# A 16-batch layer of two attentions and a routed feed-forward on one core: SyncE's, GpSimd's and the side jobs' order laid out anew, root-mean-square scaling moved to ScalarE and GpSimd

## The reference

```python
xn = layernorm(x)
# plain attention: 16 heads of 8, no rotation
q, k, v = split(xn @ Wqkv.T)
out_a = softmax_clipped(q @ k.T / sqrt(8)) @ v @ Wout.T   # exp(clip(s - max, -50, 50))
# rope attention and feed-forward
q, k, v = rope(xn @ Wq), rope(xn @ Wk_c @ Wk), xn @ Wv_c @ Wv
x1 = rmsnorm(xn + softmax(q @ k.T / sqrt(8)) @ v @ Wo, norm1_w)
shared = swiglu(x1 @ W_shared_in) @ W_shared_out
# group of experts by softmax, top 2 of 4 in the group, weights w
routed = sum(swiglu(x1 @ W1_shared) @ W2[e] * w[:, e] for e in range(8))
out_f = rmsnorm(x1 + shared + routed, norm2_w)
return x + out_a + out_f
```

## Time and profile before

| | |
|---|---|
| median of three runs | 2199.28 us (2190.82 to 2200.78) |
| the profiled execution | 2193.28 us, of which 2191.5 us lie between first and last instruction |
| PE busy | 1929.2 us (88%), 10244 instructions |
| DVE busy | 1688.0 us (77%), 2933 |
| ACT busy | 1439.5 us (66%), 2967 |
| POOL busy | 1082.4 us (49%), 1663 |

### The profile page before, as it was taken

The page is one execution under the profiler, slowest core; times in us unless marked ns, Lnnn a source line. Parts: engine busy times, 40 slices in busy tenths (PEclk is TensorE's granted clock), DMA queues, the critical chain, the costliest instruction groups (busy, mean ns, idle before and its releaser), DMA issues.

```text
span 2191.5 us, 43869 instructions
## 1 busy us (share of the span) xinstructions
PE 1929.2 (88%) x10244; PEld 580.1 (26%) x10244; DVE 1688.0 (77%) x2933; ACT 1439.5 (66%) x2967; POOL 1082.4 (49%) x1663
## 2 busy tenths in 40 slices
PE   5888889898898989989898998989899898998985
PEld 1122222222222222222222222222222222222222
DVE  4888978878788887978878787777878888787612
ACT  1376766676666767666676766667666676766752
POOL 2343537264563726446373653726455372644635
PEclk7599999999999999999998999999999999999998
DMA  3122221212112121212212112121211212121010
GB/s 101 37 60 65 59 69 53 71 46 74 46 53 74 51 71 48 71 48 55 70 50 72 48 54 66 55 70 43 75 45 53 74 51 71 48 62 55 20 48 15
DMA packets 120255, 125.89 MB, mean 57 GB/s; under 512 B 35196, under 2 KB 86780, under 8 KB 119932
## 3 DMA queue, kind: packets, MB, share of 16 engines
q1 hardware_dynamic: 120072, 124.18, 19.0%
HBM read 29.11 MB, written 22.02 MB: 23 GB/s over the span
## 4 chain that ended last, share of the span: by engine, by line
PE 57%; DVE 15%; issue 9%; DMA 9%; ACT 5%; SPq 3%; POOL 2%; DVEq 1%; ACTq 0%; POOLq 0%
PE o_ps L574 17%; PE score_ps L539 14%; PE side_ps L646 10%; DVE negmax L826 7%; PE shift_ps L554 4%; ACT weights L682 4%; PE side_ps L633 2%; PE side_ps L603 2%; PE side_ps L619 2%; DMA inv_wide<-inv_rows 2%; PE side_ps L615 2%; DMA xn_old<-xn_mid 2%; DMA res_old<-res_new 2%; DVE x L856 1%; DVE weights L834 1%
## 5 line engine op out<-in xcount | busy, mean ns | idle before, releaser
L826 DVE TENSOR_REDUCE negmax<-score_ps 128x1 f32<-128x512 f32 x2048 | 1318.1, 682 | 354.9 <-PE score_ps L539 346.7
L682 ACT ACTIVATE weights<-shift_ps 128x512 f32<-128x512 f32 x2048 | 1140.7, 597 | 637.1 <-PE shift_ps L554 533.4
L539 PE MATMUL score_ps<-kt,qt 48*128 48x512 bf16 x2048 | 691.6, 404 | 99.5 <-DVE negmax L826 84.9
L554 PE MATMUL shift_ps<-qt,kt 51*128 51x512 bf16 x2048 | 709.9, 397 | 40.4 <-ACT weights L682 35.6
L574 PE MATMUL o_ps<-weights,vt 128*32 128x512 f32 x4096 | 575.0, 635 | 3.9 <-POOL weights L1027 3.5
L1027 POOL TENSOR_SCALAR weights<-weights 128x2048 f32<-128x2048 f32 x192 | 366.5, 1909 | 95.8 <-ACT weights L682 77.0
L539 PEld LDWEIGHTS score_ps<-kt,qt 48*128 48x128 bf16 x2048 | 137.8, 95 | 828.7 <-DVE negmax L826 734.0
L646 PE MATMUL side_ps<-w_sb,hidden 128*128 128x512 f32 x512 | 252.6, 619 | 2.2 <-ACT spread L716 1.3
L554 PEld LDWEIGHTS shift_ps<-qt,kt 51*128 51x128 bf16 x2048 | 155.2, 94 | 181.0 <-ACT weights L682 172.6
L716 ACT ACTIVATE spread<-side_ps,gate 128x128 f32<-128x128 f32 x512 | 159.9, 377 | 30.0 <-PE side_ps L646 22.8
L633 PE MATMUL side_ps<-x1T,w_up_sb 128*128 128x512 f32 x256 | 144.6, 650 | 2.6 <-DVE hidden L882 2.3
(11 more groups left out here) (106 smaller groups left out, 1444.7 us busy)
## 6 DMA issues: line engine op xcount, KB each, us to landing
qt<-q_parts SPq DMA_DIRECT2D x768, 32.0 KB
kt<-k_parts SPq DMA_DIRECT2D x768, 32.0 KB
o_rows<-o_sb SPq DMA_DIRECT2D x64, 256.0 KB, 2.0
swung<-turned SPq DMA_DIRECT2D x64, 128.0 KB, 2.4
heads_raw<-o_rows SPq DMA_DIRECT2D x64, 128.0 KB
inv_wide<-inv_rows SPq DMA_DIRECT2D x32, 256.0 KB, 3.3
x_in<-in_x_dram SPq DMA_DIRECT2D x16, 256.0 KB, 2.7
xn_mid<-xn_new SPq DMA_DIRECT2D x16, 256.0 KB, 2.4
```

What stands on the lines that cost most here:

```text
L539: pe.matmul(score_ps[:, score_bank(a, t), :], qt[a][row:row + HROWS, slot, 128 * tile:128 * tile + 128], kt[a][row:row + HROWS, slot, :], ...
L554: pe.matmul(shift_ps[:, t % 2, :], kt[a][row:row + HROWS + MROWS, slot, 128 * tile:128 * tile + 128], qt[a][row:row + HROWS + MROWS, slot, ...
L682: act.activation(weights[:, i % 8, tile, :], shift_ps[:, t % 2, :], ACT.Exp, scale=SCALE).then_inc(weighed, 1)
L826: dve.tensor_reduce(negmax[:, i // 8, tile, i % 8:i % 8 + 1], score_ps[:, score_bank(a, t), :], AX.X, ALU.max, negate=True).then_inc(max_t ...
```

## The change

It moves work between engines and changes the order on all of them; what is computed stays.

- **SP**, even step: `xn_old` goes ahead of `move_o(o_plain1)`, and `widen(PLAIN)` goes ahead of the store of the output and of both moves of the residual.
- **Scaling**: the eight operations of DVE per batch (four for `x1`, four for the output) are gone. ACT multiplies by the root in four activations (even beat 13, odd beat 54), and one GpSimd operation of 512 columns multiplies by the norm's weights (`norm_weight`).
- **Side jobs**: even `max_rope1` 11 to 13, `up2`, `up3` and `down1`, `down2` laid out anew, `max_plain0` 43 to 45, `down3` 45 to 49, `shared_out` 53 to 57; odd `max_plain1` 7 to 3 and ahead of `q_plain`, `k_rope` 57 to 55. By the new places `k_plain` shares its bank with `max_plain1` and not with `q_plain`.
- **Consumers**: `copy0` from 53 to 55 in both steps; `hi0`, `mid0`, `mid1`, `shares`, `square_out` and `scale_x1` by some beats.
- **GpSimd**: both steps in a new order.

```diff
-EVEN = [("v0", [1]), ("x1T", [3]), ("v1", [5]), ("gates", [9]), ("max_rope1", [11]), ("up0", [13]), ("down0", [17]),
-        ("up1", [21]), ("down1", [25]), ("up2", [29]), ("down2", [33]), ("up3", [37]), ("y_plain", [41]),
-        ("max_plain0", [43]), ("down3", [45]), ("shared_out", [53])]
-ODD = [("xnT", [1]), ("q_plain", [5]), ("max_plain1", [7]), ("k_plain", [9]), ("exp0", [13]),
-       ("exp1", [17]), ("exp2", [21]), ("exp3", [25]), ("exp4", [29]), ("exp5", [33]), ("exp6", [37]), ("y_rope", [41]),
-       ("max_rope0", [43]), ("exp7", [45]), ("q_rope", [53]), ("k_rope", [57])]
+EVEN = [("v0", [1]), ("x1T", [3]), ("v1", [5]), ("gates", [9]), ("max_rope1", [13]), ("up0", [13]), ("down0", [17]),
+        ("up1", [21]), ("up2", [25]), ("up3", [29]), ("down2", [33]), ("down1", [37]), ("y_plain", [41]),
+        ("max_plain0", [45]), ("down3", [49]), ("shared_out", [57])]
+ODD = [("xnT", [1]), ("max_plain1", [3]), ("q_plain", [5]), ("k_plain", [9]), ("exp0", [13]), ("exp1", [17]),
+       ("exp2", [21]), ("exp3", [25]), ("exp4", [29]), ("exp5", [33]), ("exp6", [37]), ("y_rope", [41]),
+       ("max_rope0", [43]), ("exp7", [45]), ("q_rope", [53]), ("k_rope", [55])]
...
-AT = {"merge": 40, "invert": 27, "hi0": 7, "hi1": 9, "mid0": 13, "mid1": 17, "copy1": 21, "copy0": 53, "z": 33, "shares": 34, "top": 28,
-      "square_x1": 46, "scale_x1": 55, "square_out": 6, "scale_out": 13, "stats": 44, "moments": 51, "norm": 59}
+AT = {"merge": 40, "invert": 27, "hi0": 5, "hi1": 9, "mid0": 10, "mid1": 25, "copy1": 21, "copy0": 55, "z": 33, "shares": 33, "top": 28,
+      "square_x1": 46, "scale_x1": 54, "square_out": 5, "scale_out": 13, "stats": 44, "moments": 51, "norm": 59}
```

The new functions, `scale` on ACT and `norm_weight` on GpSimd:

```diff
+            def scale(b, dst, which, lag):
...
+                if live(b, lag):
+                    act.wait_ge(rms_done, norms_done(b, lag, which) + 1)
+                    for tile in range(NT):
+                        scaling = act.activation(dst[:, tile, :], dst[:, tile, :], ACT.Copy,
+                                                 scale=rms[:, which, tile:tile + 1])
+                    scaling.then_inc(rms_used[which], 1)
...
+            def norm_weight(b, dst, which, lag, signal):
...
+                if live(b, lag):
+                    pool.wait_ge(rms_used[which], cnt(b, lag, 1, 1))
+                    pool.tensor_tensor(dst[:], dst[:], norm_sb[:, which, :].unsqueeze(1).broadcast_to([128, NT, 128]),
+                                       ALU.mult).then_inc(signal, 1)
```

SP's even step, with `widen` now behind the load of `x_in`, and a few lines of GpSimd's odd one:

```diff
                     sp.dma_start(x_in[:], x[b + 1]).then_inc(x_landed, 16)
+                widen(b, PLAIN)
...
                     sp.dma_start(res_new[:], x[b + (-1)]).then_inc(res_landed, 16)
-                widen(b, PLAIN)
...
             def odd(b):
+                clip(b, 0)
                 split_max(b, "max_plain1")
-                clip(b, 0)
...
-                divide(b, ROPE)
+                clip(b, 6)
                 split_max(b, "max_rope0")
                 clip(b, 8)
                 mix(b, 5)
...
+                divide(b, ROPE)
+                square_x1(b)
```

More of the change, by code:

```diff
@@ L849, in add_side @@
                 dve.tensor_tensor(dst, tiles(bank(job)), other, ALU.add).then_inc(free(job), 1)
[L851 to L858, removed]
             def mean_square(b, which, lag):
@@ L1014, in root @@
             def root(b, lag, which):
+                if not live(b, lag):
+                    return
                 pool.wait_ge(summed, norms_done(b, lag, which) + 1)
@@ L1030, in router @@
             def router(b, first):
+                if not live(b, -2):
+                    return
                 k = [0 if first else ROUTE_A]
@@ L1125, in third, with square_out, finish, square_x1 @@
                                        ALU.subtract).then_inc(lo_done[a], 1)
-            def even(b):
-                turn(b, 0)
-                turn(b, 1)
+            def square_out(b):
                 if live(b, -3):
                     pool.tensor_tensor(square, out_sb[:], out_sb[:], ALU.mult).then_inc(squared, 1)
-                split_max(b, "max_rope1")
-                rope_less_first(b, 0, q_rest, q_parts)
+            def finish(b):
                 if live(b, -3):
[L1135 to L1138, removed]
+                    norm_weight(b, out_sb, 1, -3, scaled)
+                    pool.wait_ge(scaled, cnt(b, -3, 1, 1))
                     pool.wait_ge(res_moved, cnt(b, -3, 16, 16))
                     pool.tensor_tensor(out_sb[:], out_sb[:], res_old[:], ALU.add).then_inc(final_done, 1)
[L1141 to L1146, removed]
+            def square_x1(b):
+                if live(b, -1):
+                    taken(pool, b, "y_rope")
+                    pool.tensor_tensor(square, x1[:], x1[:], ALU.mult).then_inc(squared, 1)
+            def spread_of_x(b):
                 if live(b, 1):
@@ L1153, in even @@
                     pool.tensor_tensor(ln_rstd[:, :], ln_var[:, :], minus_half[:, :], ALU.pow).then_inc(rstd_done, 1)
-                if live(b, -2):
-                    router(b, False)
+            def even(b):
+                split_max(b, "max_rope1")
+                square_out(b)
+                turn(b, 0)
+                turn(b, 1)
+                root(b, -3, 1)
+                rope_less_first(b, 0, q_rest, q_parts)
+                rope_less_first(b, 1, k_rest, k_parts)
+                third(b, 0, ROPE, 0, q_rest, q_parts)
+                router(b, True)
+                finish(b)
+                split_max(b, "max_plain0")
+                third(b, 0, ROPE, 1, k_rest, k_parts)
+                divide(b, PLAIN)
+                router(b, False)
+                spread_of_x(b)
                 place_v(b, PLAIN)
             def odd(b):
+                clip(b, 0)
                 split_max(b, "max_plain1")
-                clip(b, 0)
                 clip(b, 1)
-                third(b, 1, PLAIN, 0, q_rest, q_parts)
                 third(b, 1, PLAIN, 1, k_rest, k_parts)
                 clip(b, 2)
+                clip(b, 4)
+                third(b, 1, PLAIN, 0, q_rest, q_parts)
                 mix(b, 0)
-                clip(b, 4)
+                clip(b, 5)
                 mix(b, 1)
-                clip(b, 5)
                 mix(b, 2)
-                clip(b, 6)
                 mix(b, 3)
                 mix(b, 4)
-                divide(b, ROPE)
+                clip(b, 6)
                 split_max(b, "max_rope0")
@@ L1176, in odd @@
                 mix(b, 5)
-                if live(b, -1):
-                    taken(pool, b, "y_rope")
-                    pool.tensor_tensor(square, x1[:], x1[:], ALU.mult).then_inc(squared, 1)
+                divide(b, ROPE)
+                square_x1(b)
                 clip(b, 9)
-                if live(b, -1):
-                    root(b, -1, 0)
                 mix(b, 6)
                 clip(b, 10)
+                root(b, -1, 0)
                 mix(b, 7)
-                place_v(b, ROPE)
+                norm_weight(b, x1, 0, -1, x1_done)
                 clip(b, 12)
                 clip(b, 13)
+                place_v(b, ROPE)
                 clip(b, 14)
```

13 lines of the change are left out of this document (7 added, 6 removed).

## The result

The changed kernel takes **2307.69 us** (median of four runs, 2295.26 to 2318.47) where the kernel before takes 2200.03 us (four runs, 2190.82 to 2203.16): a ratio of 1.049, with a 95% interval of 1.043 to 1.055. It is slower, as forecast, but by 107.7 us and not by 50; the time lies above the range.

What follows compares the result with a forecast made beforehand. PE was taken as the bound (57% of the last-ending chain), with DVE at the odd step's end. Terms of -69, +73, +83 and -36 made +51 us, so 2250 us from the 2199.28 median; range 2205 to 2295.

Steps and rivals of the forecast that it cites:

- (a): `y_plain` at even beat 41: earlier `widen` removes PE's 4.10 us wait and its low clock, -5.6 us a pair.
- (e): Odd step's end: DVE loses four operations of 1007 ns, -3.7 us; ACT's four activations take about 1.15 us.
- (f): Beat 55: PE's `value` waits for the later `copy0`, +1.3 us an even step and +2.1 an odd one.
- (c): `k_plain` in the odd step: on another bank its wait goes, -1.25 us a pair.
- other places: New places of `up`, `down`, `shared_out` and other edits: costed at nothing, could be 0.6 us either way.
- (b): Odd beat 3: the split for `max_plain1` behind a clip makes PE wait 4.3 us, +5.8 with the clock.
- (d): Odd beat 41: late division delays `headsT`, PE waits 4.35 us, +5.9 with the clock, 14 times.
- 1.5 us of low clock: Price charged behind every PE wait of some 4 us, on top of its idle time.
- The rival with one wait missing: Only one of the odd step's two long waits comes, 2167 or 2157 us; chance 0.09 for one or none.
- that with waits free of clock: Both long odd-step waits come but cost only their idle time, 2205 us; chance 0.12.
- that of a late `y_plain`: Even beat 41: GpSimd's `headsT` ends 2 us after PE arrives, 2300 us; chance 0.11.
- the 86 named as a sign: Sign in the profile after: DVE busy 64 + 22 us less.

Runs made afterwards that it cites:

- e7: Kernel before with SP's two edits alone (`xn_old` and `widen` earlier), GpSimd's order as before: 2131.33 us, ratio 0.969 to before.
- e8: Kernel before with the scaling alone moved to ACT and GpSimd, `copy0` still at beat 53: 2149.58 us, ratio 0.977 to before.
- e12: e11 with one line more, odd `max_plain1` at beat 5 ahead of `q_plain`: 2056.36 us, ratio 0.937 to before.
- e11: Kernel before with SP's early spreading and the scaling on ACT and GpSimd, nothing else: 2071.80 us, ratio 0.943 to before.
- e4: Changed kernel with `copy0` at 53, GpSimd's split ahead of the clip and its division right behind expert 4's mix: 2054.34 us, ratio 0.933 to before.
- e2: Changed kernel with GpSimd's split for `max_plain1` ahead of the clip of head 0 again: 2225.18 us, ratio 1.010 to before.
- e3: Changed kernel with GpSimd's division for rope attention right behind the mix of expert 4 again: 2240.57 us, ratio 1.018 to before.
- e1: Changed kernel with `copy0` at beat 53 again in both steps: 2215.74 us, ratio 1.007 to before.
- e5: Changed kernel with unread products filling PE's four waits of a pair, no wait removed: 2219.69 us, 88 us less than the changed kernel.
- e10: Changed kernel with split and division undone but `copy0` left at beat 55: 2148.98 us, ratio 0.978 to before.

## Why the direction was right and the size was not

By the steps of the prediction, in us of the middle, where both profiles of before agree to 0.1:

| term | predicted | measured | from |
|---|---|---|---|
| (a) `widen` | -90 | -61.1 | e7 |
| (e), (f) scaling with its gaps | -67 | -52.5 | e8 |
| (c) `k_plain` | -20 | -19.9 | e12 - e11 |
| other places | 0 | -10.3 | e4 - e12 |
| (a) and scaling together | 0 | -10.2 | e11 against e7 and e8 |
| (b) `max_plain1` | +93 | +99.9 | e2 |
| (d) division | +83 | +74.4 | e3 |
| (f) copies | +52 | +98.3 | e1 |
| overlap of the three | 0 | -12.7 | e4 against e1, e2, e3 |
| sum | +51 | +105.9 | |

- **The step that failed** is the sentence that charged the 1.5 us of low clock "behind every wait of some 4 us", and so not behind the waits for the copies in (f). Their idle time was nearly right (predicted 1.3 and 2.1 us, 1.18 and 2.63 in the rows, 1.1 and 2.5 in e5). But the clock fell behind them as well, which e10 shows with these waits alone: 99.3 us in the middle for 54.9 us of waiting. 31 waits at 1.5 us are 46 us; with them the sum is 97, against 106 measured. That the rest is only 9 us is luck: it is a balance of misses of up to 29 us with both signs.
- **The price itself was right on the mean.** Filling four waits a pair took 96.3 us from the middle: 1.55 us each for 62 waits (16 splits, 15 divisions, 31 copies). By place it was not: 0.7 to 2.5 us.
- **(b) and (d)** were right in place, releaser and idle time: 4.21 and 4.23 us of idle time in the rows, 4.3 and 4.35 predicted. The rival with one wait missing is out by the wait table, that with waits free of clock by e5, that of a late `y_plain` by the 1.8 us of margin.
- **(a)** was right at its beat (5.7 us a pair for 5.6) and 29 us too high over the run. Of these some 10 are the blocked operation at beat 34 and another 10 the longer low stretch from the end of the odd step, which come back in the joint term of the table.
- **(e)** The scaling's total came near, its working did not: -3.7 us was DVE's time alone, and the end of the odd step held a low stretch besides, whose loss reaches into the next even step, while even beats 16 to 23 were to stay as they were and took 13.3 us more. DVE's busy time fell by 74 us (1688.0 to 1614.1), not by the 86 named as a sign. Four activations took 1.26 us, for my 1.15. The Trainium skill's budget (ScalarE: Activation LUTs, Rules for kernel authors) gave an estimate of 1.6 us for four. One does take 0.39 us here; in a row they overlap, so four times the budget is too high.
- **The tail** was costed at nothing. It is 19 us longer in the changed kernel's profile, and 8.5 us also appear without any edit. The run profiled of the changed kernel is the longest of its four (2318.47 us), so that middle and tail together show somewhat more than the medians do.

## What to carry to other kernels

Price every new wait of the engine that bounds the kernel, the short ones too, as its idle time plus the slow stretch behind it: here waits of 1.2 to 4.2 us cost 1.5 us more each on the mean (0.7 to 2.5 by place), and the 31 short ones, 44 us by e10, were what my sum had left out. Look for such stretches in the kernel before as well; a part of their loss lies in the beats behind them. Moving work off the critical engine is only worth it if the order around it keeps the jobs that this engine waits for ahead of those it doesn't: three swaps in the queues of ACT and GpSimd separate 2308 from 2054 us with the same work. And where a wait can't be removed, useless work in it may pay.

## What the runs showed of the hardware

- Products that nobody reads, put into PE's waits, made the kernel 88 us (3.8%) faster. The Trainium skill (TensorE: Matmul & The Clock Gate, Part 1) holds that the throttled state is the default and that activity releases it. The trace of e5 agrees: the granted clock of its middle steps is 1.00, where the changed kernel had 0.93 over a pair.
- The length of a wait doesn't decide alone. The clock fell behind 1.18 us at even beat 55, but in e11, whose middle steps have no low stretch, PE still waits 1.25 us for `k_plain` 16 times in the odd step:

```profile
PE side_ps L616 <- DVE q_rest L943: 19.7, 16, 1.4
```

- A GpSimd operation on 512 columns stretched a DVE operation on 4 columns from 0.16 to 0.94 us.
- Two profiles of one kernel agreed to 0.1 us over 2025 us and differed by 8.5 us in the 130 behind it, where the granted clock was at 1.00 in one and 0.50 in the other for 20.4 us.
